# Eight places for returning rows, and scatters of the second half in two of three scan steps

## The chip, the cores and the metric

One core of one Trainium2 chip. The time is the device time of the slowest core in microseconds, here of the only one; the median of the runs is quoted. Engines are named as in the profile: PE (TensorE), DVE (VectorE), ACT (ScalarE), POOL (GpSimd), SP (SyncE). A name ending in q is the instruction queue of an engine, from which DMAs are issued.

## What is computed

The input x has 8 sequences of 512 tokens with 128 channels. After a layer norm two branches run on the same tokens. One is a state-space scan, 512 steps long in the reference, with a layer norm in each step; the other is a mixture of 8 experts, two for each token. The output is x plus the product of both.

```python
def step(state, bc):
    b_t, c_t = bc
    s = state @ A_bar + b_t
    s = _layernorm(s, ln_st_g, ln_st_b)
    return (s, c_t * s)
...
h = _gelu(jnp.einsum('bsd,edh->ebsh', xn, ew1) + eb1[:, None, None, :])
eo = jnp.einsum('ebsh,ehd->ebsd', h, ew2) + eb2[:, None, None, :]
moe_out = jnp.einsum('ebsd,bse->bsd', eo, w_dense)
for i in range(NROT):
    moe_out = moe_out @ expm(gens[i])
...
x = x + s * g
```

Only the two best experts of a token have a weight in `w_dense`, so the kernel computes those two alone.

## The kernel before

**The scan.** Each sequence is cut into 16 segments (`SEG`) of 32 steps (`L`); all 128 segments (8 x 16) are advanced side by side, one on each partition. As the start of a segment is the end of the one before it, the 32 steps are run in five rounds (`ROUNDS`) that improve the starts. The first round begins at its step 12. This makes 148 scan steps, `STEPS`, counted by t from 0. Step t is: VectorE transposes the state (L949), TensorE multiplies it (L1047, 16 small matmuls, semaphore `product`), VectorE finds the root for the layer norm and writes the next state (L961). Rounds end at t = 19, 51, 83 and 115, with two more matmuls and a chain on VectorE (`vector_boundary`).

**The experts.** The 8192 pairs of token and expert are sorted by expert, in two halves of 39 tiles with 128 rows each (`HALF_TILES`, `TILES` = 78). A `scatter` on GpSimd (L1701) is an indirect DMA that writes 128 rows of 129 words (66 KB) to their sorted places in DRAM, `sorted_rows0` for the first half and `sorted_rows1` for the second. There are 64, 32 for each half. Eight go out ahead of the scan (`SCATTER_LEAD`); the others are issued inside the steps, each after that step's `product`.

The tiles are computed in between the scan steps. `SLOT_AT` gives a slot j to four of five steps from t = 26 on, to t = 126. In slot j TensorE does `layer1(j - 2)`, `rows_transpose(j)` and `layer2(j - 3)`, and ScalarE does `gelus(j - 2)`, `rows_transposed(j)` and `rows_copied(j - 3)`. The last of these (L1612) copies the finished tile g from PSUM into place g % `OUT_PLACES` of `rows_out`; it first waits until the scatter that last used this place has landed. From there `rows_back(g)` on GpSimd (L1715), an indirect DMA of 66 KB as well, sends the rows back to the order of the tokens. It stands one step behind the slot. Every third slot GpSimd also computes row numbers (`row_numbers`, L1708). Each engine works through its instructions in the order in which they are written, whatever else is ready.

**SyncE's queue.** `fetch(g)` (L1749) loads the weights of tile g's expert, a record of 290.5 KB, into one of five places once `layer2(g - 5)` is done. It first reads the expert's number into a register. `load_rows(c)` (L1759) loads the sorted rows of three tiles, 193.5 KB, at most three chunks ahead. For c = 0 it waits for all scatters of the first half, for c = 13 (tiles 39 to 41) for all scatters of the second half. SyncE's order is `fetch(35)`, `load_rows(13)`, `fetch(36)`, `fetch(37)`, `fetch(38)`, `load_rows(14)`. Tile 36's record is used by `layer1(36)` in slot 38, at t = 73; tile 39's rows by `rows_transpose(39)` in slot 39, at t = 74.

**Later.** `pull` (L1771) brings the returned rows of a half back into SBUF once all of them have landed, VectorE and ScalarE mix them from t = 82 on, and the output is stored at the end. VectorE also waits for all second-half scatters at t = 116, where the last round begins to write into their source.

Of the kernel before, what the change touches and what calls it, by code (L numbers as in the profile page):

```python
# [19 lines left out]
SEG = 16  # L20
ROUNDS = 5
RECORDS = 5
OUT_PLACES = 5
FIRST_STEP = 12
MAGIC_ROUNDS = 2
TOLERANCE = 1e-5
# [13 lines left out]
def build(nc, I, out):  # L40
    NB, T, H = I["L0_attn_x"].shape
    S = I["L0_attn_A"].shape[0]
    E, _, F = I["L0_ffn_ew1"].shape
    NROT = I["L0_ffn_gens"].shape[0]
    K = F // P
# [5 lines left out]
    Q = NS // HALVES  # L51
# [10 lines left out]
    with ExitStack() as ctx:  # L62
        sems = {}

        def sem(name):
            if name not in sems:
                sems[name] = ctx.enter_context(nc.semaphore(name))
            return sems[name]

        def sb(name, shape, dt=F32):  # L70
            return ctx.enter_context(nc.sbuf_tensor(name, shape, dt))
# [43 lines left out]
        gi = sb("gi", [P, NB, T])  # L115
        rows_out = sb("rows_out", [P, OUT_PLACES, W])
        bias_words = gi[0:3, :, :].rearrange("p b t -> p (b t)")
# [284 lines left out]
        def eb2_split(pool, j):  # L402

            x = eb2r[:, :] if j == 0 else eb2_rest[:, j - 1]
            pool.wait_ge(sem("eb2_copied"), 1)
            if j:
                pool.wait_ge(sem("eb2_parts"), 2 * j)
            pool.tensor_copy(eb2_part[:, j, 0:W], x).then_inc(sem("eb2_parts"), 1)
            if j < 2:
                pool.wait_ge(sem("eb2_parts"), 2 * j + 1)  # L410
                pool.tensor_tensor(eb2_rest[:, j], x, eb2_part[:, j, 0:W], ALU.subtract).then_inc(sem("eb2_parts"), 1)
# [718 lines left out]
        def fallback(eng, one_round, redo):  # L1130

            eng.wait_ge(sem("agreed"), 1)
            settled = eng.value_load(agreed[0:1, 0:1], min_val=0, max_val=1)
            with eng.If(settled < 1):
                if one_round is not None:
                    with eng.Fori(0, SEG) as r:
                        one_round(eng, r)
                redo(eng)
            eng.end_ifs()
# [7 lines left out]
        STEPS = (L - FIRST_STEP) + (ROUNDS - 1) * L  # L1147

        def round_of(t):
            r, k = divmod(t + FIRST_STEP, L)  # L1150
            return r, k, t + 1 + r
# [18 lines left out]
        C_AT = {23: 0, 30: 1, 45: 2, 60: 3, 75: 4, 90: 5, 105: 6, 120: 7}  # L1170
        ROTATED = 14
        SCATTER_LEAD = 8
        MIX_AT = [84, 91, 98, 105, 131, 134, 137, 140]
        VALUES_PER_STEP = [2, 2, 2, 2]
        SUMMED = NB // 2
# [4 lines left out]
        def out_bank(g):  # L1180
            return banks[3 + g % 2][:, 0:W]
# [4 lines left out]
        def value_steps(n):  # L1186
            if n >= SUMMED:
                return MIX_AT[n] + 5, MIX_AT[n] + 8
            return MIX_AT[n] + 5, MIX_AT[n] + 5 + (3 * SUB + VALUES_PER_STEP[n] - 1) // VALUES_PER_STEP[n]

        scaled_rows = [desk[:, i * T:(i + 1) * T].rearrange("p (s h) -> p s h", s=SUB) for i in range(2)]

        def scaled_part(act, n, part):
            _, _, _, a, rest_g = factors(n)
            j = 3 * (n - SUMMED) + part
            if part == 0:
                act.wait_ge(sem("factor"), 5 * n + 5)
            if j >= 2:
                m, p = divmod(j - 2, 3)
                if p == 2:  # L1200
                    act.wait_ge(sem("ffn"), SUMMED + m + 1)
                else:
                    act.wait_ge(sem("summed"), 2 * m + p + 1)
            for s in range(SUB):
                row = pulls[:, n % 4, s, part, 0:P] if part < 2 else abel[:, n, s, :]
                scale = a[:, s, part:part + 1] if part < 2 else rest_g[:, s:s + 1]
                t = act.activation(scaled_rows[j % 2][:, s, :], row, ACT.Copy, scale=scale)
            t.then_inc(sem("scaled"), 1)
# [64 lines left out]
        def vector_mix(dve, n, t):  # L1273

            at = t - MIX_AT[n]
            first, end = value_steps(n)
# [14 lines left out]
        def scalar_mix(act, n, t):  # L1291

            _, u, th, _, _ = factors(n)
            v = values[n % 4]
            if t == MIX_AT[n] - 2:
                if n >= 4:
# [4 lines left out]
                i.then_inc(sem("mix_rows"), 1)  # L1301
            elif t == MIX_AT[n] + 2:
                act.wait_ge(sem("factor"), 5 * n + 3)
# [65 lines left out]
        def residual(pool, again, n):  # L1369
            pool.wait_ge(sem("gated_ssm"), NB * again + n + 1)  # L1370
            pool.tensor_tensor(outb[:, n], outb[:, n], X[:, n * SUB:(n + 1) * SUB, :], ALU.add).then_inc(sem("final_rows"), 1)  # L1371
# [38 lines left out]
        with nc.Block() as block:  # L1410
# [142 lines left out]
            def _(act):  # L1553
# [54 lines left out]
                def rows_copied(g):  # L1608
                    act.wait_ge(sem("rows_done"), g + 1)
                    if g >= OUT_PLACES:  # L1610
                        act.wait_ge(sem(f"rows_out{g % OUT_PLACES}"), 16 * (g // OUT_PLACES))
                    act.copy(rows_out[:, g % OUT_PLACES, :], out_bank(g)).then_inc(sem("rows_copied_out"), 1)  # L1612

# [82 lines left out]
            @block.gpsimd  # L1696
            def _(pool):
                def scatter(i):
                    h, i = divmod(i, 2 * Q)
                    q, j = h * Q + i // 2, i % 2  # L1700
                    pool.indirect_dma_start(sorted_rows[h], bass.IndirectOffsetOnAxis(ap=slots[:, j, q:q + 1], axis=0), sort_rows[:, q, :], None)\  # L1701
                        .then_inc(sem(f"scattered{h}"), 16)

                def row_numbers(c):
                    mine = slice(c * CHUNK, (c + 1) * CHUNK)
                    here = slice((c % 3) * CHUNK, (c % 3 + 1) * CHUNK)
                    pool.wait_ge(sem(f"rows_in{c % 3}"), 16 * (c // 3 + 1))
                    pool.tensor_tensor(token_rows_i[:, mine], row_numbers_in[:, here].squeeze(2), row_shift_i[:, mine], ALU.add)\  # L1708
                        .then_inc(sem("token_rows"), 1)

                def rows_back(g):
                    h = g // HALF_TILES
                    pool.wait_ge(sem("token_rows"), g // CHUNK + 1)
                    pool.wait_ge(sem("rows_copied_out"), g + 1)
                    pool.indirect_dma_start(token_rows[h], bass.IndirectOffsetOnAxis(ap=token_rows_i[:, g:g + 1], axis=0), rows_out[:, g % OUT_PLACES, :], None)\  # L1715
                        .then_inc(sem(f"rows_out{g % OUT_PLACES}"), 16)

                front_gpsimd(pool)
                pool.sem_inc(sem("stored"), 2)
                pool.wait_ge(sem("rows_cleared"), 16 * HALVES)  # L1720
                pool.wait_ge(sem("slots_ready"), 1)
                for i in range(SCATTER_LEAD):
                    scatter(i)
                for t in range(STEPS):
                    r, k, turn = round_of(t)
                    if SCATTER_LEAD + t < 4 * Q:
                        pool.wait_ge(sem("product"), turn)
                        scatter(SCATTER_LEAD + t)
                    if EB2_AT < t <= EB2_AT + 3:
                        eb2_split(pool, t - EB2_AT - 1)  # L1730
                    j = SLOT_AT.get(t - 1)
                    if j is not None and 3 <= j:
                        rows_back(j - 3)
                    j = SLOT_AT.get(t)
                    if j is not None and j < TILES and j % CHUNK == 0:
                        if j == 0:
                            pool.wait_ge(sem("tables"), 10)
                        row_numbers(j // CHUNK)
                for n in range(NB - 3, NB):
                    residual(pool, 0, n)  # L1740
                fallback(pool, pool_round, pool_redo)
# [83 lines left out]
```

## Time and profile before

| | us |
|---|---|
| Median of 3 runs | 410.24 (409.66 to 414.73) |
| The profiled execution's own time | 405.85 |
| Its span, first to last instruction | 404.0 |
| GpSimd's indirect DMAs for the scatters, 64 | 63.8 busy |
| GpSimd's indirect DMAs for the returning rows, 78 | 75.8 busy |
| TensorE's mean granted clock | 0.92 of full speed |

The profile shows one execution. In the timelines a row has a start in microseconds from the start of the span, a duration, the engine, the line and the operation; a bracket behind it gives the idle time of the engine just before and who ended it. DMA rows on GpSimd and SyncE are the time that the engine needs to issue them; the data land later. Step t of the scan can be found by its transpose: L949 occurs 148 times, in the order of t.

### The profile page before, as it was taken

To read this page: it belongs to the slowest core of one execution; us is meant where nothing else is said; L and a number is where in the kernel's file an instruction comes from. 1 tells how busy PE (TensorE), PEld (TensorE's weight loads), DVE (VectorE), ACT (ScalarE), POOL (GpSimd) and SP (SyncE) were. 2 spreads that over 40 slices of the span, in tenths; PEclk is the share of its full clock that TensorE was granted. 3 is DMA by queue.
4 is the path that set the end of the run, shared out by engine and by line. 5 is a ranking of instruction groups with operands and counts; after the bars stand their busy time and mean duration, and the time that the engine had idled before them with its cause. 6 is when DMAs were issued, how large, how long until landed. Compare 5 with 4: busy or idle time off the path is not lost.

```text
span 404.0 us, 11723 instructions
## 1 busy us (share of the span) xinstructions
PE 327.0 (81%) x4029; PEld 244.4 (60%) x4029; DVE 284.0 (70%) x1357; ACT 195.2 (48%) x587; POOL 188.8 (47%) x261
## 2 busy tenths in 40 slices
PE   2897983997787569996997999999997989887670
PEld 1676941775564347875865877877866765443340
DVE  2547589869877547876553666689999567799970
ACT  1217730201322326673636676587775573587510
POOL 8408950725546437777777545345544251000110
PEclk9999986799989959999898999899999899999955
DMA  8199950411110345665564668866656222600001
GB/s 255 22 190 163 135 117 0 130 35 36 41 40 29 140 123 187 231 222 184 189 195 158 219 192 261 280 215 203 210 178 219 79 92 56 228 28 27 28 29 55
DMA packets 44158, 54.81 MB, mean 136 GB/s; under 512 B 6840, under 2 KB 28767, under 8 KB 44095
## 3 DMA queue, kind: packets, MB, share of 16 engines
q1 hardware_dynamic: 38975, 42.52, 37.7%
q0 software_dynamic: 4544, 9.39, 7.1%
q10 hardware_dynamic: 576, 2.10, 1.5%
q8 instruction: 35, 0.57, 0.6%
q14 instruction: 28, 0.23, 0.2%
HBM read 14.15 MB, written 16.63 MB: 76 GB/s over the span
## 4 chain that ended last, share of the span: by engine, by line
PE 40%; DVE 32%; POOL 8%; issue 8%; DMA 6%; ACT 2%; SPq 2%; POOLq 0%; DVEq 0%; ACTq 0%
PE bank L1478 8%; PE bank L1047 7%; PE bank L1488 5%; DVE wT L949 4%; DVE ring L961 3%; DVE roots L914 3%; DMA token_rows<-rows_out,token_rows_i 3%; DVE sqj L938 2%; PE bank L465 2%; PE bank L492 2%; POOL sorted_rows L1701 2%; POOL late L307 2%; DVE xpad L1254 2%; DVE Rho L916 2%; PE bank L1471 2%
## 5 line engine op out<-in xcount | busy, mean ns | idle before, releaser
L1715 POOL DMA_INDIRECT token_rows<-rows_out,token_rows_i x78 | 75.8, 972 | 71.9 <-ACT rows_out L1612 47.6
L1701 POOL DMA_INDIRECT sorted_rows<-late,slots x64 | 63.8, 997 | 56.6 <-PE bank L1047 34.3
L1047 PE MATMUL bank<-Mrep,wT 32*32 32x64 f32 x2368 | 65.9, 226 | 18.8 <-DVE wT L949 18.0
L1047 PEld LDWEIGHTS bank<-Mrep,wT 32*32 32x32 f32 x2368 | 42.2, 108 | 52.6 <-issue 49.3
L1605 ACT ACTIVATE desk<-bank,record 128x128 f32<-128x128 f32 x156 | 48.9, 366 | 36.1 <-PE bank L1478 35.6
L961 DVE SCALAR_TENSOR_TENSOR ring<-bank,Rho,Dv 128x64 f32<-128x64 f32 x112 | 31.6, 282 | 40.5 <-PE bank L1047 38.6
L1478 PE MATMUL bank<-desk,record 128*128 128x128 f32 x312 | 58.5, 313 | 0.0
L1488 PE MATMUL bank<-record,desk 128*128 128x129 f32 x312 | 50.2, 285 | 0.0
L1478 PEld LDWEIGHTS bank<-desk,record 128*128 128x128 f32 x312 | 43.1, 200 | 7.5 <-issue 1.0
L1488 PEld LDWEIGHTS bank<-record,desk 128*128 128x128 f32 x312 | 43.2, 201 | 0.1
L1597 ACT ACTIVATE desk<-bank,cols 128x128 f32<-128x128 f32 x78 | 36.0, 462 | 6.4 <-PE bank L1471 6.4
L1493 PE MATMUL bank<-bias,ones 128*128 128x512 bf16 x116 | 32.5, 385 | 0.0
L1471 PE MATMUL bank<-ident,desk 128*128 128x128 f32 x78 | 22.8, 293 | 11.8 <-DMA desk<-sorted_rows 6.0
L949 DVE STREAM_TRANSPOSE wT<-ring 128x64 f32<-128x64 f32 x112 | 27.5, 245 | 3.6
L1612 ACT COPY rows_out<-bank 128x129 f32<-128x129 f32 x78 | 21.3, 273 | 17.7 <-DMA token_rows<-rows_out,token_rows_i 14.6
L1371 POOL TENSOR_TENSOR xT<-xT,X 128x512 f32<-128x512 f32 x3 | 3.7, 1260 | 53.1 <-DVE xT L1366 53.1
L1471 PEld LDWEIGHTS bank<-ident,desk 128*128 128x128 f32 x78 | 11.8, 151 | 13.1 <-ACT desk L1597 6.3
L938 DVE CUSTOM_DVE_ANT_0 sqj<-ring,guess 128x64 f32<-128x64 f32 x64 | 19.6, 306 | 0.1
L914 DVE SCALAR_TENSOR_TENSOR roots<-z_all 128x1 f32<-128x1 f32 x96 | 16.0, 166 | 3.3
L916 DVE SCALAR_TENSOR_TENSOR Rho<-roots,Rho 128x1 f32<-128x1 f32 x96 | 15.5, 161 | 3.3
L1489 PE MATMUL bank<-record,ones 128*128 128x129 bf16 x78 | 17.8, 228 | 0.0
L594 ACT ACTIVATE gi<-bank,cols 128x512 f32<-128x512 f32 x8 | 5.5, 687 | 22.9 <-PE bank L458 22.9
(328 smaller groups left out, 658.8 us busy)
## 6 DMA issues: line engine op xcount, KB each, us to landing
record<-experts SPq DMA_DIRECT2D x78, 290.5 KB
sorted_rows<-zero_rows SPq DMA_DIRECT2D x2, 2515.5 KB, 26.6
desk<-sorted_rows SPq DMA_DIRECT2D x26, 193.5 KB
pulls<-token_rows SPq DMA_DIRECT2D x8, 516.0 KB, 5.2
X<-in_L_attn_x ACTq DMA_DIRECT2D x4, 512.0 KB, 5.5
out<-xT SPq DMA_DIRECT2D x8, 256.0 KB, 2.0
token_rows<-rows_out,token_rows_i POOLq DMA_INDIRECT x78
experts<-in_L_ffn_ew SPq DMA_DIRECT2D x1, 1024.0 KB, 28.1
```

Of the source, the lines that this page charges most:

```text
L914: dve.scalar_tensor_tensor(out=w_now, in0=z, scalar=linear, in1=z, op0=ALU.add, op1=ALU.mult).then_inc(sem("root_w"), 1)
L949: dve.transpose(wT[:, :], prev).then_inc(sem("state_T"), 1)
L961: dve.scalar_tensor_tensor(out=state(r, k), in0=psY, scalar=Rho[:, k:k + 1], in1=Dv[:, k, :], op0=ALU.mult, op1=ALU.add).then_inc(sem("sta ...
L1047: t = pe.matmul(psY[q], wT[q, 32 * c:32 * c + 32], Mrep[q, c, :], start=(c == 0), stop=(c == 1))
L1471: pe.transpose(bank_in[:, 0:P], rows_in[:, g % (3 * CHUNK), 0:P], ident[:, :]).then_inc(sem("rows_seen"), 1)
L1478: t = pe.matmul(hidden_bank(g)[:, k * P:(k + 1) * P], w[:, k * P:(k + 1) * P], rows_T[:, g % 2, :], start=True, stop=True)
L1488: pe.matmul(o, hidden[:, g % 2, k, :], w[k], start=(k == 0), stop=False)
L1493: pe.matmul(banks[bank][:, :], ones_all3[:, :], bias_all3[:, 1].rearrange("p s h -> p (s h)"), start=True, stop=True)
L1597: act.activation(rows_T[:, g % 2, :], bank_in[:, 0:P], ACT.Identity, scale=col["ln_gamma"], bias=col["ln_beta"]).then_inc(sem("rows_T"), 1)
L1605: t = act.activation(hidden[:, g % 2, k, :], hidden_bank(g)[:, k * P:(k + 1) * P], ACT.Gelu, bias=bias[:, k:k + 1])
L1701: pool.indirect_dma_start(sorted_rows[h], bass.IndirectOffsetOnAxis(ap=slots[:, j, q:q + 1], axis=0), sort_rows[:, q, :], None)\
L1715: pool.indirect_dma_start(token_rows[h], bass.IndirectOffsetOnAxis(ap=token_rows_i[:, g:g + 1], axis=0), rows_out[:, g % OUT_PLACES, :], N ...
```

## The change

Two things. `OUT_PLACES` goes from 5 to 8, so ScalarE waits for the landing of tile g - 8 in place of g - 5. And the second half's scatters are no longer issued one in each step up to t = 55: up to t = 23 nothing changes, from t = 24 on a step divisible by three has none. The last one is then in t = 71. Their number and their data stay the same.

```diff
-OUT_PLACES = 5
+OUT_PLACES = 8
...
         SCATTER_LEAD = 8
+        SCATTER_AT = {}
+        for t in range(STEPS):
+            if SCATTER_LEAD + len(SCATTER_AT) < 4 * Q and (t < 2 * Q - SCATTER_LEAD or t % 3):
+                SCATTER_AT[t] = SCATTER_LEAD + len(SCATTER_AT)
...
-                    if SCATTER_LEAD + t < 4 * Q:
+                    if t in SCATTER_AT:
                         pool.wait_ge(sem("product"), turn)
-                        scatter(SCATTER_LEAD + t)
+                        scatter(SCATTER_AT[t])
```

GpSimd's order before, from t = 53 to the first steps without a scatter. `sorted_rows` rows are scatters, `token_rows` rows are returning rows.

```order
L1701 DMA sorted_rows<-late,slots 4992x129
L1715 DMA token_rows<-rows_out,token_rows_i 9089x129
L1701 DMA sorted_rows<-late,slots 4992x129
L1715 DMA token_rows<-rows_out,token_rows_i 9089x129
L1701 DMA sorted_rows<-late,slots 4992x129
L1715 DMA token_rows<-rows_out,token_rows_i 9089x129
L1708 TENSOR_TENSOR token_rows_i<-desk,row_shift_i 128x3
L1715 DMA token_rows<-rows_out,token_rows_i 9089x129 x3
L1708 TENSOR_TENSOR token_rows_i<-desk,row_shift_i 128x3
```

The last scatter stands behind 20 returns. The same engine after the change, from t = 70, past the last scatter in t = 71 (lines are shifted by 4):

```order
L1705 DMA sorted_rows<-late,slots 4992x129
L1719 DMA token_rows<-rows_out,token_rows_i 9089x129
L1705 DMA sorted_rows<-late,slots 4992x129
L1712 TENSOR_TENSOR token_rows_i<-desk,row_shift_i 128x3
L1719 DMA token_rows<-rows_out,token_rows_i 9089x129 x3
L1712 TENSOR_TENSOR token_rows_i<-desk,row_shift_i 128x3
L1719 DMA token_rows<-rows_out,token_rows_i 9089x129 x3
```

The last scatter now stands behind 33 returns. Between the second return and the last scatter there were 22 scatters, 19 returns (that second one counted) and 6 computations of row numbers; there are now 25, 32 and 10.

SyncE's order has not moved; this is the place in it with the load of tiles 39 to 41, and what it waits for:

```order
L1753 DMA record<-experts 128x581
L1763 DMA desk<-sorted_rows 128x3x129 [waits token_rows,rows_seen,scattered1]
L1750 TENSOR_LOAD expert_of
L1750 ISA x2
L1753 ISA [waits rows_done]
L1753 DMA record<-experts 128x581
```

The record in the first row is tile 35's, the one in the last row tile 36's.

## Rows read from the trace of the kernel before

**Rows 1.** The profile's page: busy time of each engine
```profile
PE 327.0 (81%) x4029; PEld 244.4 (60%) x4029; DVE 284.0 (70%) x1357; ACT 195.2 (48%) x587; POOL 188.8 (47%) x261
```
**Rows 2.** Waits of ACT, 150 to 214 us: total, times, longest
```profile
ACT rows_out L1612 <- DMA token_rows<-rows_out,token_rows_i: 14.6, 9, 3.2
```
**Rows 3.** The chain that ended last, in order of time
```profile
180.52 3.93 DMA token_rows<-rows_out,token_rows_i
```
**Rows 4.** Timeline of POOL, 157 to 223 us
```profile
157.42 0.96 POOL L1715 DMA_INDIRECT token_rows<-rows_out,token_rows_i  x1 [0.30 <-issue]
...
159.95 0.96 POOL L1715 DMA_INDIRECT token_rows<-rows_out,token_rows_i  x1 [0.30 <-issue]
160.94 0.20 POOL L1708 TENSOR_TENSOR token_rows_i<-desk,row_shift_i 128x3 int32<-128x3 int32 x1
161.30 0.99 POOL L1701 DMA_INDIRECT sorted_rows<-late,slots  x1 [0.16 <-issue]
...
209.96 0.96 POOL L1701 DMA_INDIRECT sorted_rows<-late,slots  x1 [0.30 <-issue]
...
222.75 0.96 POOL L1715 DMA_INDIRECT token_rows<-rows_out,token_rows_i  x1 [0.94 <-ACT rows_out L1612]
```
**Rows 5.** Timeline of DVE, transposes of steps 44, 66, 73, 82, 83, 84
```profile
174.12 0.24 DVE L949 STREAM_TRANSPOSE wT<-ring 128x64 f32<-128x64 f32 x1
222.25 0.24 DVE L949 STREAM_TRANSPOSE wT<-ring 128x64 f32<-128x64 f32 x1
233.52 0.25 DVE L949 STREAM_TRANSPOSE wT<-ring 128x64 f32<-128x64 f32 x1
248.85 0.25 DVE L949 STREAM_TRANSPOSE wT<-ring 128x64 f32<-128x64 f32 x1
250.46 0.24 DVE L949 STREAM_TRANSPOSE wT<-ring 128x64 f32<-128x64 f32 x1
254.90 0.25 DVE L949 STREAM_TRANSPOSE wT<-starts 128x64 f32<-128x64 f32 x1
```
**Rows 6.** Timeline of SP's queue; 227.14 is load_rows(13)
```profile
159.43 0.53 SPq L1759 DMA_DIRECT2D desk<-sorted_rows  x1
160.99 4.92 SPq L1749 DMA_DIRECT2D record<-experts  x3
...
174.07 2.96 SPq L1749 DMA_DIRECT2D record<-experts  x3
...
227.14 0.52 SPq L1759 DMA_DIRECT2D desk<-sorted_rows  x1
```
**Rows 7.** DMA issues (KB each, us to landing), and L1701's durations
```profile
pulls<-token_rows SPq DMA_DIRECT2D x8, 516.0 KB, 5.2
out<-xT SPq DMA_DIRECT2D x8, 256.0 KB, 2.0
L1701 POOL DMA_INDIRECT sorted_rows<-late,slots x64: 957/961/1454, 70.3 to 210.0; - x64
DMA to landing us min/median/max: 2.3/2.4/5.6
L1701 POOL DMA_INDIRECT sorted_rows<-late,slots x27: 957/962/997, 149.6 to 210.0; - x27
```
**Rows 8.** Timeline of PE: a slot step at half clock and one at full
```profile
216.78 0.65 PE L1047 MATMUL bank<-Mrep,wT 32*32 32x64 f32 x16
219.69 0.49 PE L1047 MATMUL bank<-Mrep,wT 32*32 32x64 f32 x16
...
232.62 0.43 PE L1047 MATMUL bank<-Mrep,wT 32*32 32x64 f32 x16
234.24 0.43 PE L1047 MATMUL bank<-Mrep,wT 32*32 32x64 f32 x16
234.59 0.71 PE L1478 MATMUL bank<-desk,record 128*128 128x128 f32 x4
```
**Rows 9.** Stretches: length, busy (x) of PE, PEld, DVE, ACT, POOL, PEclk, DMA share, GB/s
```profile
139.00:145.00 6.00, 0.24 (x1) 0.18 (x1) 1.22 (x8) 0.47 (x3) 1.11 (x2) 0.70 0.80 261
145.00:147.00 2.00, 1.59 (x32) 0.96 (x33) 0.94 (x6) 0.92 (x2) 0.92 (x2) 0.50 0.27 77
147.00:151.00 4.00, 4.00 (x41) 3.33 (x34) 3.13 (x19) 1.52 (x6) 2.23 (x4) 0.50 0.11 35
...
213.00:216.00 3.00, 0.32 (x3) 0.12 (x3) 0.95 (x6) 2.83 (x9) 2.39 (x3) 1.00 0.70 209
216.00:220.00 4.00, 4.00 (x48) 3.24 (x48) 1.08 (x6) 2.31 (x8) 3.19 (x5) 0.57 0.35 126
```

## The prediction

> **What bounds the kernel now.** I read the busy times first: TensorE is busy 81% of the span and no other engine over 70% [rows 1], so the question is where TensorE stands still. Then ScalarE's waits between 150 and 214 us: nine times, 14.6 us together, the copy into a returning place (L1612) waits for the row scatter that still holds the place [rows 2]. The same view from 214 us on has no such wait, so all nine lie in the stretch where GpSimd issues both kinds of scatter. The chain that ended last shows one of them: a scatter issued at 180.52 is passed on only 3.93 us later [rows 3].
>
> The timeline of GpSimd says why. From 157.42 us on it issues one indirect DMA after another. Check with the program order: from the second `rows_back` (157.42) to the last `scatter` (209.96) it has 19 + 22 DMAs and 6 short `row_numbers` to pass [rows 4]. A pair with `row_numbers` between them takes 161.30 - 159.95 = 1.35 us; 41 DMAs at 1.266 and 6 times 0.09 give 52.4 us, and 209.96 - 157.42 is 52.5. So GpSimd does not wait at all there: it is a server at 1.27 us a DMA. A group of five scan steps gives it 5 scatters and 4 returns, 9 x 1.27 = 11.4 us; TensorE needs 1.66 us a step when nothing holds it ((248.85 - 222.25) / 16) [rows 5], 8.3 us for the five. GpSimd is the slower one until its scatters end; at 222.75 it waits again for ScalarE [rows 4]. With five places TensorE can't run far ahead, so it takes GpSimd's pace: step 44 starts at 174.12, step 73 at 233.52 [rows 5], 2.05 us a step.
>
> **The change, part by part.**
> *Eight places.* The nine waits go, or nearly: GpSimd's lag may grow to eight slots. Undisturbed, the 29 steps from 44 to 73 take 29 x 1.66 = 48.2 us, and a round boundary inside them (step 52) adds what the one at step 84 adds, 254.90 - 250.46 less 1.66, some 2.8 us [rows 5]. TensorE would come to step 73 at 174.1 + 51.0 = 225.1 in place of 233.5: 8.4 us early. That is the gain on offer, if nothing else stands in the way. Memory apart, this edit adds no instruction.
>
> *The scatters of the second half spread to step 71.* None is removed. GpSimd now gets 10 scatters and 12 returns in 15 steps, 22 x 1.27 = 27.9 us against TensorE's 24.9: still the slower one, by 3 us per 15 steps. So it still never waits, and the time of the last scatter is a count. From the second `rows_back`, whose predecessors in the order are all waiting for TensorE as before and which I therefore leave at 157.42, the order has 32 returns, 25 scatters and 10 `row_numbers` in front of the last scatter: 57 x 1.266 + 10 x 0.09 = 73.1 us, so it starts at 230.5 us, 20.5 us later than before. The 13 returns that now stand before it are 16.5 us of this, three postponed scatters the rest. The fixed spacing excludes more than a microsecond less; more is possible, as a scatter took up to 5.6 us to land in place of 2.4 [rows 7]. I keep -1 to +2 us.
>
> *Who waits for the last scatter.* `load_rows(13)`, the first one of the second half, waits for all 32 scatters of that half, and it stands in SyncE's order directly ahead of `fetch(36)`. Before, the scatters had landed at 212.4 (209.96 + 2.4) and this load went out at 227.14 without waiting for them [rows 6]: 14.7 us of cover, which the move uses up. Behind the waiting load stand `fetch(36)`, (37), (38) and the next load; TensorE needs the first of them in step 73, and ScalarE and the scan stop with it. GpSimd's returns for tiles already computed go on. Now: 230.5 + 2.4 to landing [rows 7] = 232.9; the load's issue takes 0.53; from its end to the next fetch's issue another 1.03 (159.43 + 0.53 to 160.99) [rows 6]: `fetch(36)` at 234.5. Its landing is not listed. From below, the 256 KB store of the output lands in 2.0 us; from above, a 516 KB pull in 5.2 [rows 7]. A record has 290.5 KB, next to the store; I take 2.5 because the 193.5 KB of `load_rows(13)` move just before it. So the record of tile 36 is there at 237.0. TensorE used it at 234.59 (L1478 in step 73) [rows 8]: +2.4 us. The rows of tile 39, needed one step later, leave 1.6 us before the record and are hidden behind it. Further records follow each other at (2.96 - 0.50) / 2 = 1.23 us [rows 6], faster than TensorE's slots, so SyncE catches up and adds nothing.
>
> The Trainium skill, "DMA: Bandwidth & Descriptors", section on the anatomy of a DMA issued from GpSimd, gives each DMA a fixed 2.0 us and the bytes over 436 GB/s. Taken for the record that would be 2.7 us where I take 2.5, and 2.15 us for a 66 KB scatter where the trace has 2.4. An estimate by that page for both makes the gate +2.35 in place of +2.4; the 5.2 of the trace for 516 KB is 2 us above what it gives for that size (3.2), so the trace is not always as quick as the rule, and the upper end stays.
>
> *TensorE stands idle before that.* It comes to step 73 at about 225 and goes on at 237: 12 us without a matmul. In this trace its clock falls to the lower of its levels (1.2 of 2.4 GHz) around such stops: from 139 to 145 us it was busy for 0.24 us, and the granted clock is 0.50 from 145 to 151; from 213 to 216 it was busy for 0.32 us, and the clock is 0.57 from 216 to 220 [rows 9]. A step with a slot takes 219.69 - 216.78 = 2.91 us there and 234.24 - 232.62 = 1.62 at full clock [rows 8], 1.3 us more. The shortest such period held one and a half of these steps, the longest, 145 to 151 and a little more, would hold a little over two. I take 1.7 steps, +2.2 us; the ends are +1.3 and +3.9 (three steps). Before had its own slow period at 216, but that one lies ahead of the gate and gives nothing back.
>
> *After step 74* every step keeps its order. The ScalarE waits were gone there already, so eight places have nothing left to give, and the shift of step 74 runs to the end. The early part up to step 23 is untouched, and so is the first half's load.
>
> **Sum.** The 8.4 us gained before step 73 are spent waiting for the gate, and the gate opens later than before: +2.4 + 2.2 = +4.6 us. On the profiled execution (span 404.0, 405.85 us in all, so 1.85 lie around the span) that is 410.5. The runs shown have a median of 410.24, 4.4 above that execution; the prediction is for such a median: 410.24 + 4.6 = 414.8, 1.1% more. Ends of the sum: GpSimd -1, record 2.0, clock 1.3 gives +2.2; +2, 5.2 and 3.9 give +11.0, an unlikely corner.
>
> **Rivals.**
> *The gate hides nothing (faster).* If the last scatter were issued by about 218.5, the record would be there at 225 and the 8.4 us would stay: 401.8. For it: TensorE really has that much room. Against: GpSimd would have to pass 57 DMAs in 61 us, 1.07 us each, and all of its steady rows have 1.26 to 1.27. 4%.
> *The gate opens just where TensorE was before.* The record lands in 2.0 us, GpSimd is a microsecond early because the returns now come without a late copy, and the clock comes back after one step: +1 or less, 410 to 411.5. 18%.
> *The slow clock stays (slower).* After the gate TensorE could go on at half clock up to the next round boundary at step 84, if short stops between late records keep it from rising: 8 slot steps at 1.3 us, +10.4, with +2.4 for the gate 423. It decides from 4.5 slow steps on, where the sum passes 2%. For it: records 36 to 38 come one by one just then, beside rows and returns, which kept the DMA engines 0.70 busy in the stop at 213 [rows 9]. Against: 1.23 us between records is less than a step, and both periods in the trace ended within 7 us. 13%.
> *The DMAs on GpSimd get longer (slower).* With TensorE undisturbed, VectorE's scan work is denser beside GpSimd's DMAs. The longest scatter of the trace took 1.454 us against a median of 0.961 [rows 7]; were all 57 as long, the gate would open 57 x 0.49 = 28 us later: 443. Against: between 150 and 212 us, with the scan running, the 27 scatters took 957 to 997 ns [rows 7]. 2%.
> The Trainium skill, "SBUF — State Buffer", section "Who interferes with whom", has such a rule: GpSimd is starved of port time for writing its DMAs' descriptors while VectorE holds the port pair that the two share. No row of this stretch shows it at work.
>
> **How the numbers follow.** The forecast (+2 to +8) has 63%, the rivals in their order 4, 18, 13 and 2. About 2% (8.2 us) is what a measurement of this kernel can tell from no change. Faster by more: only the first rival, 0.04. Slower by more: the last two, 0.15. The rest, 0.81: two chances in ten of it lie at or near no change. The range reaches from the second rival to a gate late by most of its bounds (+10.3), and leaves out the far ends: 410.0 to 420.5.
>
> **What would show it.** Right: no ScalarE wait for returning rows; the last second-half scatter at 230 to 232; the load behind it at 233; TensorE idle some 12 us in step 73, ended by the load or record, with a granted clock near 0.5 behind it; the transpose of step 84 some 4 to 5 us later than 254.90. Wrong: GpSimd with idle time between 160 and 230, a spacing other than 1.27, a record in use before 235, or step 84 earlier than before.

## The result, and the profile after

The changed kernel has a median of 413.47 us (20 runs), the kernel before 408.54 (20 runs). The ratio is 1.0129, with a 95% interval of 1.0088 to 1.0169: slower by 1.3%, within the 2% that count as no change. This ratio, and each one below, is taken from each kernel's fast runs alone (those within 1.5% of its fastest), so it differs a little from the quotient of the medians (1.0121). The prediction was 414.8 us, 1.1% more than before. The profiled execution has a span of 407.7 us against 404.0.

ScalarE's waits between 150 and 214 us. The row that stood in [rows 2], a copy waiting for a place, is gone; only a wait for TensorE's result is left at L1616 (L1612 before). The first row is the largest of ScalarE's waits there, at `gelus`:

```profile
ACT desk L1609 <- PE bank L1482: 15.4, 21, 3.9
...
ACT rows_out L1616 <- PE bank L1493: 0.6, 3, 0.2
```

GpSimd's timeline: the second return, the last scatter, and the first return that again had to wait for ScalarE. These answer to [rows 4]:

```profile
158.29 0.96 POOL L1719 DMA_INDIRECT token_rows<-rows_out,token_rows_i  x1 [0.30 <-issue]
...
231.91 0.96 POOL L1705 DMA_INDIRECT sorted_rows<-late,slots  x1 [0.31 <-issue]
...
241.37 0.96 POOL L1719 DMA_INDIRECT token_rows<-rows_out,token_rows_i  x1 [5.86 <-ACT rows_out L1616]
```

The last scatter starts at 231.91, 21.95 us later than in [rows 4]. SyncE's queue is next, its waits first (total, times, longest). A load has waited 12.0 us for scatters, once:

```profile
SPq L1763 <- DMA sorted_rows<-late,slots: 12.0, 1, 12.0
```

In the timeline it is the load at 234.20, `load_rows(13)`, with `fetch(36)` and two more behind it. Nothing leaves the queue between 222.1 and 234.2:

```profile
217.14 4.95 SPq L1753 DMA_DIRECT2D record<-experts  x3
234.20 0.37 SPq L1763 DMA_DIRECT2D desk<-sorted_rows  x1
235.45 2.85 SPq L1753 DMA_DIRECT2D record<-experts  x3
```

TensorE's timeline shows what that costs. The product of step 73 is computed at 229.30; then comes `layer1(36)`, after 8.18 us of idle time that the record ends. The products of steps 74 and 75 follow:

```profile
229.30 0.42 PE L1047 MATMUL bank<-Mrep,wT 32*32 32x64 f32 x16
237.91 1.22 PE L1482 MATMUL bank<-desk,record 128*128 128x128 f32 x4 [8.18 <-DMA record<-experts]
...
240.24 0.65 PE L1047 MATMUL bank<-Mrep,wT 32*32 32x64 f32 x16
...
242.33 0.42 PE L1047 MATMUL bank<-Mrep,wT 32*32 32x64 f32 x16
```

The matmuls behind the stop take 1.22 us where they take 0.71 at full clock [rows 8]. The stretches (columns as in [rows 9]) show the granted clock, 0.50 and then 0.66:

```profile
236.00:238.00 2.00, 0.09 (x1) 0.09 (x1) 0.00 (x0) 0.00 (x0) 0.00 (x0) 0.50 0.70 258
238.00:240.00 2.00, 2.00 (x10) 1.94 (x10) 0.00 (x0) 0.83 (x3) 0.00 (x0) 0.50 0.78 273
240.00:242.00 2.00, 2.00 (x26) 1.59 (x25) 0.57 (x3) 0.59 (x3) 0.63 (x1) 0.66 0.69 230
242.00:244.00 2.00, 2.00 (x24) 1.11 (x23) 1.51 (x10) 1.11 (x5) 0.82 (x3) 1.00 0.70 246
```

And the transposes of steps 44, 73 and 84, beside those in [rows 5]:

```profile
174.92 0.25 DVE L949 STREAM_TRANSPOSE wT<-ring 128x64 f32<-128x64 f32 x1
...
228.65 0.24 DVE L949 STREAM_TRANSPOSE wT<-ring 128x64 f32<-128x64 f32 x1
...
259.75 0.24 DVE L949 STREAM_TRANSPOSE wT<-starts 128x64 f32<-128x64 f32 x1
```

So step 44 is 0.8 us later than before (0.6 of it is there from step 0 on, 88.08 against 87.47), step 73 is 4.9 us earlier, and step 84 is 4.85 us later. The gain is there at step 73; the wait inside that step spends all of it, and more.

### The profile page after: what moved, and what is told of

Its sections match the earlier page's. It is cut to its first block, busy times and chain, and to the rows that moved or that the text cites. A ratio compares the mean times of both kernels' runs of the same rounds, so it can differ in the third digit from the quotient of the medians.

```text
span 407.7 us, 11723 instructions
## 1 busy us (share of the span) xinstructions
PE 326.9 (80%) x4029; PEld 243.9 (60%) x4029; DVE 284.3 (70%) x1357; ACT 195.0 (48%) x587; POOL 189.0 (46%) x261
## 4 chain that ended last, share of the span: by engine, by line
PE 43%; DVE 31%; issue 8%; POOL 6%; DMA 6%; ACT 2%; SPq 2%; DVEq 0%; POOLq 0%; ACTq 0%
PE bank L1482 9%; PE bank L1047 8%; PE bank L1492 6%; DVE wT L949 4%; DVE ring L961 3%; DVE roots L914 2%; DVE sqj L938 2%; PE bank L465 2%; PE bank L492 2%; DVE Rho L916 2%; DVE xpad L1258 2%; PE bank L419 2%; PE bank L1475 2%; POOL sorted_rows L1705 1%; PE bank L1467 1%
## 5 line engine op out<-in xcount | busy, mean ns | idle before, releaser
L1047 PE MATMUL bank<-Mrep,wT 32*32 32x64 f32 x2368 | 66.0, 226 | 18.7 <-DVE wT L949 17.6
L1047 PEld LDWEIGHTS bank<-Mrep,wT 32*32 32x32 f32 x2368 | 42.2, 107 | 52.4 <-issue 49.2
L1497 PE MATMUL bank<-bias,ones 128*128 128x512 bf16 x116 | 33.8, 397 | 0.0
L1616 ACT COPY rows_out<-bank 128x129 f32<-128x129 f32 x78 | 21.4, 274 | 2.8 <-PE bank L1493 2.8
L1497 PEld LDWEIGHTS bank<-bias,ones 128*128 128x128 bf16 x116 | 9.8, 100 | 10.8 <-issue 1.8
```

The costliest lines, as they stand in the source:

```text
L1047: t = pe.matmul(psY[q], wT[q, 32 * c:32 * c + 32], Mrep[q, c, :], start=(c == 0), stop=(c == 1))
L1497: pe.matmul(banks[bank][:, :], ones_all3[:, :], bias_all3[:, 1].rearrange("p s h -> p (s h)"), start=True, stop=True)
```

## The experiments

The theory under test: the time is set by a gate. `load_rows(13)` waits for the last scatter; that scatter's start is a count of DMAs at 1.27 us; SyncE's queue passes the wait on to record 36 and so to TensorE. The main rival: the loss comes with the eight places, or from how much each engine does at once, and the wait is only what the trace names.

Four runs went first to a chip on which the kernel before had a median of 454.6 us (445.6 to 457.6, 11 runs). They are told at the end of this section; the same kernels were run again on other chips, and those runs decide.

### One part alone: eight places

```diff
-OUT_PLACES = 5
+OUT_PLACES = 8
```

> Edit: eight places alone, again, as the first run of it had a kernel before of 454.6 us beside it, 46 us over the median known, with TensorE waiting for its own instructions in the profile. Gate theory, where the kernel before takes 403 to 412 us: last scatter near 210 us, ScalarE's waits for places under 6 us, step 73 4 to 8 us earlier than before; ratio 0.980 to 0.990. Rival (places bring nothing or cost): 1.00 to 1.01.

Measured: 403.02 us against 407.59, ratio 0.990 (0.983 to 0.997). The scatter that ends the row is again at its old time, and from 150 to 300 us ScalarE waits for no place; this is GpSimd's row, and then all of TensorE's waits between 150 and 300 us:

```profile
210.04 0.95 POOL L1701 DMA_INDIRECT sorted_rows<-late,slots  x1 [0.31 <-issue]
```
```profile
PE bank L1052 <- DVE ends L971: 3.5, 2, 1.9
PE bank L1471 <- ACT desk L1597: 0.9, 1, 0.9
PE bank L1478 <- DMA record<-experts: 0.7, 2, 0.5
PE bank L1047 <- DVE wT L949: 0.5, 1, 0.5
```

Step 73 comes at 227.5 us, 6.0 us earlier than before, and step 84 still is 6.1 us earlier. The eight places gain what this experiment expected (4 to 8 us), less than the 8.4 of the prediction; the ratio stands at the weak end of the expected range. The trace shows why in part: of the 6.1 us 3.1 are left at step 147 (377.0 against 380.1), and the span ends 3.7 us earlier. Step 119 loses 1.3 us and step 147 another 1.85; ahead of the latter the granted clock is 0.56 from 370 to 375 us, where the kernel before has 1.00 up to 380. Whether another execution would lose them too is not tested.

### The other part alone: the spread

The changed kernel with

```diff
-OUT_PLACES = 8
+OUT_PLACES = 5
```

> Edit: the spread alone, five places, again. Gate theory: last scatter at 231 to 233 us, record of tile 36 at 237 to 238, ratio 1.009 to 1.017 as the changed kernel. Rival (the loss comes with the places): under 1.005.

Measured: 412.81 against 407.59, ratio 1.013 (1.007 to 1.020), the changed kernel's own. The last scatter starts at 234.22 and the record is used at 240.27, both later than expected (231 to 233, 237 to 238): this execution, of 415.0 us, began its tile loop later, see the table below. The wait for the record is there, longer:

```profile
240.27 1.22 PE L1482 MATMUL bank<-desk,record 128*128 128x128 f32 x4 [10.72 <-DMA record<-experts]
```

The rival falls: the loss comes with the spread alone, and next to it five or eight places make no difference. Even with five places ScalarE waits for none in this kernel, as GpSimd has fewer DMAs in each step, and step 73 comes at 228.5 us, where the changed kernel has 228.65. So the sum of the parts is not the whole: -1.0% and +1.3% apart, +1.3% together. Either part alone takes ScalarE's waits away, so next to the spread the places have nothing to add; and what is gained ahead of the gate, by either, is spent at the gate.

### The count changed: three of four steps

```diff
-... t < 2 * Q - SCATTER_LEAD or t % 3):
+... t < 2 * Q - SCATTER_LEAD or t % 4):
```

> Edit: the changed kernel with scatters in three of four steps from step 24 on. The last one is in step 66 with 29 returns ahead of it in place of 33, and 62 in place of 67 row of DMAs and row numbers. Gate theory: it starts 4 x 1.27 = 5 us earlier than the changed kernel's, near 227, the record of tile 36 comes near 233, and the ratio to before is 0.997 to 1.004. Rival (the price is not set by the count): ratio 1.009 or more, as the changed kernel.

Measured: 406.90 against 406.90, ratio 0.999 (0.995 to 1.003). GpSimd, then SyncE, then TensorE:

```profile
226.88 0.96 POOL L1705 DMA_INDIRECT sorted_rows<-late,slots  x1 [0.31 <-issue]
```
```profile
229.18 0.37 SPq L1763 DMA_DIRECT2D desk<-sorted_rows  x1
230.33 2.95 SPq L1753 DMA_DIRECT2D record<-experts  x3
```
```profile
233.06 1.22 PE L1482 MATMUL bank<-desk,record 128*128 128x128 f32 x4 [5.34 <-DMA record<-experts]
```

Each of these times is 4.9 to 5.1 us earlier than in the changed kernel, where the count gives 5.2. Record 36 is used 1.5 us earlier than in the kernel before, and the clock behind the stop takes that back: step 84 comes 0.8 us later (255.71). This execution took 410.31 us, 3.4 over its kernel's median. This is the sharpest test, since one number of the edit changes: four returns fewer stand ahead of the last scatter, and the ratio is 1.4 points under the changed kernel's, though taken on another chip.

### The queue changed: two fetches ahead of the load

The changed kernel, SyncE's loop:

```diff
+                LATE = HALF_TILES - 3 * CHUNK
                 for g in range(TILES):
                     if g + RECORDS < TILES:
                         fetch(g + RECORDS)
-                    if g % CHUNK == 0 and g // CHUNK + 3 < TILES // CHUNK:
+                    if g == LATE + 2:
+                        load_rows(LATE // CHUNK + 3)
+                    if g != LATE and g % CHUNK == 0 and g // CHUNK + 3 < TILES // CHUNK:
                         load_rows(g // CHUNK + 3)
```

> Edit: fetches of records 36 and 37 ahead of the load of tiles 39 to 41, again. Gate theory: step 74's transpose of rows resumes at about 236.5 us in place of a resumption of step 73 at 237.9, step 75 comes 3 to 5 us earlier than in the changed kernel, ratio 1.000 to 1.006. Rival (the order of the queue is not what costs): 1.009 to 1.017.

Measured: 410.07 against 407.59, ratio 1.0057 (1.0013 to 1.0102), inside the expected range. TensorE now passes step 73 and stops one step later, at the rows of tile 39:

```profile
237.83 0.48 PE L1475 MATMUL bank<-ident,desk 128*128 128x128 f32 x1 [7.45 <-DMA desk<-sorted_rows]
...
239.21 0.65 PE L1047 MATMUL bank<-Mrep,wT 32*32 32x64 f32 x16
```

Tile 39's rows were used at 237.83, 1.3 us later than expected; 0.9 of it is the later last scatter. The product of step 75 (second row) comes 6.4 us after the start of the last scatter (232.79), in the changed kernel 10.4 us (231.91 to 242.33). By step 80 2.7 of these 4.0 us are left, counted from the last scatter (248.5 against 250.3 at the transpose): the half clock now falls on large products behind step 75's (two 128x512 matmuls of L1447, 2.08 us where the changed kernel takes 1.13). So two waits stand behind one gate, the last scatter: the record's, and behind it that of tile 39's rows, which comes up once the record's is gone. About half of the loss stays with it.

### The clock: TensorE kept busy in the stop

The changed kernel with 36 matmuls more, 128x512 each, whose results nobody reads:

```diff
                     if t in SLOT_AT:
                         j = SLOT_AT[t]
+                        if j == HALF_TILES - 1:
+                            keep_warm(36, 1)
                         if 2 <= j < TILES + 2:
                             layer1(j - 2)
```

> Edit: the changed kernel with 36 more matmuls in slot 38, in the idle time before record 36; again, as the first run of it had a kernel before of 454.6 us beside it. Clock theory: granted clock near 1.0 from the arrival of record 36 on, and step 75 follows 1 to 2 us sooner after that arrival; the ratio is 0.002 to 0.005 under that of the changed kernel on the same chip. Rival (the clock is not what costs): the same ratio within 0.001.

> The changed kernel itself, beside e4r_kept_warm on one chip as its yardstick: ratio to before 1.009 to 1.017 by every theory.

Measured on one chip: 409.95 with them and 412.18 without, against 407.57 for the kernel before; ratios 1.0029 (0.9985 to 1.0073) and 1.0090 (1.0049 to 1.0131). TensorE with them (35 of the 36 are in the trace):

```profile
227.43 7.72 PE L1497 MATMUL bank<-bias,ones 128*128 128x512 bf16 x35 [0.16 <-issue]
236.66 0.71 PE L1482 MATMUL bank<-desk,record 128*128 128x128 f32 x4 [1.52 <-DMA record<-experts]
...
239.56 0.42 PE L1047 MATMUL bank<-Mrep,wT 32*32 32x64 f32 x16
```

```profile
236.00:240.00 4.00, 3.33 (x53) 2.83 (x53) 1.05 (x6) 2.11 (x8) 0.69 (x1) 1.00 0.69 230
```

The granted clock is 1.00 behind the stop, and from record 36 to the product of step 75 it takes 2.90 us (236.66 to 239.56) in place of 4.42 (237.91 to 242.33): the clock's price is 1.5 us in that execution of the changed kernel. It is not the same in each. From the first use of record 36 to the transpose of step 80:

| execution | us | over the kernel before |
|---|---|---|
| before (no stop) | 10.89 | |
| kept warm | 10.89 | 0.0 |
| changed | 12.42 | 1.5 |
| changed, again | 13.04 | 2.2 |
| three of four | 13.24 | 2.4 |
| spread alone | 13.73 | 2.8 |

With TensorE kept busy the price is gone to the last hundredth. In the ratios the difference is 0.6%, a little over the expected 0.2 to 0.5 (2.2 us, as in the execution of the changed kernel on this chip, would be 0.5%), and the two intervals overlap; the traces are the better evidence. The rival that VectorE's chain is what is late there falls by the 2.90.

### Scatters forward in place of back

Two in each of steps 1, 3, 5, 6, 7 and 9, three in each of steps 24 to 26, one in the others, up to step 43; with eight places, and with five:

```diff
+            last = min(first + (2 if t in (1, 3, 5, 6, 7, 9) else 3 if t in (24, 25, 26) else 1), 4 * Q)
+            SCATTER_AT[t] = range(first, last)
```

> Edit: eight places; the second half's scatters are moved forward in place of back: two in each of steps 1, 3, 5, 6, 7 and 9, three in each of steps 24 to 26, where GpSimd has idle time, and one in the others. The last one is in step 43 with 10 returns ahead of it in place of 33. Gate theory: the last scatter starts before 185 us, nothing waits for it, ScalarE has almost no wait for a place (under 2 us), step 73 comes 5 to 9 us earlier than in the kernel before; ratio to before 0.975 to 0.988. Rival (GpSimd's lateness only moves elsewhere, to the start of the tile loop or to the later returns): ratio over 0.992.

> Edit: as e5_early_8 with five places. If the surplus of DMAs on GpSimd inside the tile loop is what fills the places, moving 12 scatters (15 us of GpSimd) forward takes most of the waits away without more places: ratio 0.980 to 0.993, and what eight places add to it is under 0.6%. Rival (five places are too few at any pace of GpSimd): ratio over 0.995, with ScalarE waiting more than 8 us for places.

Measured: with eight places 401.61 against 406.90, ratio 0.988 (0.981 to 0.995); with five 404.73, ratio 0.986 (0.977 to 0.995). GpSimd's last scatter of the first of them, and ScalarE's waits for places in the second, 3.7 us in place of 14.6:

```profile
183.83 0.95 POOL L1707 DMA_INDIRECT sorted_rows<-late,slots  x1 [0.30 <-issue]
```
```profile
ACT rows_out L1618 <- DMA token_rows<-rows_out,token_rows_i: 3.7, 3, 2.2
```

With eight places ScalarE has no wait for one. One expectation was missed: step 73 comes at 229.85 us with eight places, 3.7 earlier than before in place of 5 to 9. The execution was 1.7 us late from step 0 on (89.16 against 87.47), and the granted clock fell to 0.50 behind the round boundary of step 52, as in item 3 of the account below.

Both are faster than both kernels of the case, by less than 2%. The surplus of DMAs on GpSimd inside the tile loop filled the places; fewer DMAs there or more places to hold them each take most of the waits away. Of the three ways to faster (places alone 0.990, forward with eight 0.988, with five 0.986) none can be told from the others. Forward has a price of its own: the row numbers for the first tiles are computed at 147.56 in place of 144.85 us, behind the nine scatters of steps 24 to 26; 1.7 of these 2.7 us are the later start of the execution.

### The count over all executions

For each execution whose profile was taken on a chip other than the slow one: the start of the second return, the DMAs and row numbers ahead of the last scatter by the program's order, that count at 1.266 and 0.09 us, the time measured, and how long after the last scatter's start tile 36's first matmul started, where it waited for the record.

| kernel | second return | DMAs, row numbers | count gives | measured | last scatter to record in use |
|---|---|---|---|---|---|
| before | 157.42 | 41, 6 | 52.4 | 52.5 | no wait |
| changed | 158.29 | 57, 10 | 73.1 | 73.6 | 6.00 |
| changed, again | 161.15 | 57, 10 | 73.1 | 73.1 | 6.07 |
| spread alone | 161.15 | 57, 10 | 73.1 | 73.1 | 6.05 |
| kept warm | 157.34 | 57, 10 | 73.1 | 73.2 | 6.17 |
| fetches first | 159.71 | 57, 10 | 73.1 | 73.1 | waits for rows |
| three of four | 158.93 | 53, 9 | 67.9 | 68.0 | 6.18 |
| places alone | 157.61 | 41, 6 | 52.4 | 52.4 | no wait |
| forward, eight | 159.52 | 19, 3 | 24.3 | 24.3 | no wait |
| forward, five | 159.54 | 19, 3 | 24.3 | 24.3 | no wait |

### The chip on which all was slower

> Edit: eight places, scatters one in each step as before. Gate theory (the load of tiles 39 to 41 waits for the last scatter, whose start is a count of DMAs at 1.27 us): the last scatter stays near 210 us, its landing near 212.4 is still ahead of the load's turn, and the nine waits of ScalarE shrink from 14.6 us to under 6; step 73 comes 4 to 8 us earlier than in the kernel before and this is kept: ratio to before 0.980 to 0.990. Rival (the eight places are what costs, or bring nothing): ratio 1.00 to 1.01.

> Edit: five places, scatters in two of three steps from step 24 on. Gate theory: GpSimd has the same DMAs ahead of the last scatter as in the changed kernel, so it starts at 231 to 233 us and the record of tile 36 comes at 237 to 238; ScalarE's waits for places may come back but cost nothing, and the ratio to before is that of the changed kernel, 1.009 to 1.017. Rival (each scatter less per step helps TensorE, the loss comes with the places): the ratio is under 1.005.

> Edit: the changed kernel with SyncE's fetches of records 36 and 37 put ahead of the load of tiles 39 to 41, that waits for the last scatter. Gate theory: step 73 no longer waits for its record, TensorE goes on to step 74 and stands at the rows of tile 39 in place of the record; these land at about 233.9 + 0.5 + 2.4, some 236.5 us, where the changed kernel resumed step 73 at 237.9 and had two slot steps in front of it. So step 75 comes 3 to 5 us earlier than in the changed kernel, and the ratio to before is 1.000 to 1.006. Rival (the wait for the record is only what the trace names, the time is set by GpSimd's returns or by the slow clock): ratio 1.009 to 1.017 as in the changed kernel.

> Edit: the changed kernel with 36 more matmuls of 128x512 in slot 38 on TensorE, ahead of the first matmul that needs record 36; their results are not used. They take 36 x 0.216 = 7.8 us of the 8.2 us in which TensorE stood idle. Clock theory (1.5 us of the loss are the two steps at half clock behind the idle time): granted clock 1.0 from 238 on, step 75 1 to 2 us earlier than in the changed kernel against step 73's record, ratio 0.003 to 0.005 below that of the changed kernel. Rival (the clock costs nothing since the scan's chain on VectorE is what is late there): same ratio as the changed kernel.

Measured, against 454.63 us for the kernel before: places alone 455.68, ratio 1.015 (1.005 to 1.026); spread alone 458.34, 1.023 (1.012 to 1.033); fetches first 460.39, 1.019 (1.001 to 1.037); kept warm 464.87, 1.035 (1.019 to 1.051). No ratio lies in its expected range. By these ratios eight places would be a loss, but they rest on two of the eleven runs of the kernel before (445.58 and 451.28 us); the medians give 1.002, 1.008, 1.013 and 1.023, so a change of sign is not shown. The traces show a different bound. TensorE's waits of "places alone" between 150 and 300 us, where "issue" means that no other engine and no DMA was waited for (columns as above), and a scatter on GpSimd that waited for something the trace calls remote:

```profile
PE bank L1047 <- issue: 21.3, 19, 1.8
```
```profile
234.04 0.96 POOL L1701 DMA_INDIRECT sorted_rows<-late,slots  x1 [1.05 <-remote]
```

In the traces from the other chips nothing waits for "remote", and TensorE's issue waits at L1047 are 0.4 us or less in all; the scatter that started at 234.04 here started at 210.04 there. On this chip the count does not hold, and the theory's numbers can't be read from it. In the spread kernels there the last scatter came 103 to 109 us after the second return, where the count gives 73, with many waits for TensorE and ScalarE. One reading, which an expectation above states as if the profile showed it, is that the engines get their own instructions late; the profile shows only that nothing it records was waited for. That 36 matmuls more made the worst run fits the reading, but it was not tested, and what slows that chip stays open.

## Why the prediction was right

1. *GpSimd as a server at 1.27 us a DMA.* Right: nine executions of the table agree with the count within 0.1 us, the changed kernel's first within 0.6. There GpSimd, which was to wait for nothing, waited twice for TensorE's product, behind the round boundary of step 52, while TensorE ran at half clock:

```profile
194.37 0.96 POOL L1705 DMA_INDIRECT sorted_rows<-late,slots  x1 [0.40 <-PE bank L1047]
...
197.28 0.98 POOL L1705 DMA_INDIRECT sorted_rows<-late,slots  x1 [0.46 <-PE bank L1047]
```

   The steady gaps are 0.30 and, behind row numbers, 0.16 us, so the two cost 0.4. The last scatter was said to start at 230.5 and did at 231.91; 0.87 of the difference is the later start of the second return.
2. *The gate.* Right in place, and near in price. From the last scatter's start to the record in use I had 6.5 us (230.5 to 237.0); five executions show 6.0 to 6.2. Record 36 was used at 237.91 in place of 234.59, +3.3 us against +2.4 said: the last scatter was 1.4 later than said, the stretch behind it 0.5 shorter.
3. *The gain on offer.* Mis-sized: TensorE was to come to step 73 8.4 us early and came 4.9 early (228.65 against 233.52). It started from step 44 0.8 us later, and the 29 steps from there took 53.7 us, not 51.0. Most of this lies behind the round boundary, which I had priced by the boundary at step 84. The stretches of the changed kernel show half clock for some 6 us; the last two rows are those of the spread alone, where the clock stayed up:

```profile
190.00:192.00 2.00, 1.78 (x8) 1.78 (x9) 0.69 (x7) 0.00 (x0) 1.39 (x3) 0.54 0.10 33
192.00:194.00 2.00, 2.00 (x25) 1.53 (x24) 0.21 (x1) 1.24 (x4) 1.66 (x2) 0.50 0.23 72
194.00:196.00 2.00, 2.00 (x13) 2.00 (x10) 1.02 (x6) 0.75 (x3) 1.32 (x2) 0.50 0.56 203
```
```profile
194.00:196.00 2.00, 2.00 (x32) 1.75 (x31) 1.20 (x8) 1.24 (x5) 1.39 (x3) 1.00 0.15 41
196.00:198.00 2.00, 2.00 (x31) 1.60 (x29) 1.29 (x9) 1.52 (x6) 1.70 (x2) 1.00 0.69 252
```

   TensorE stood 2.10 us at this boundary in both. In the three kernels with the spread whose clock stayed at 1.00 behind it (spread alone, fetches first, three of four) the 29 steps took 50.7, 50.7 and 50.3 us, close to the 51.0 said; why the clock fell in one execution and not in another stays open. The prediction also gave the end of ScalarE's waits to the eight places alone; the spread alone ends them too. The term stood outside the sum, since the gate decides however early TensorE comes; so the idle time was 8.2 us and not 12, and the total did not move.
4. *The clock behind the stop.* 1.5 us in the profiled execution against 2.2 said, and 2.2, 2.4 and 2.8 in three others that stop in step 73 (table above): 2.2 was a fair middle, all within the bounds (1.3 to 3.9). In the first the clock was back some 4 us after the record.
5. *The sum.* +4.6 was said; step 84 is 4.85 us later, 0.6 of it from the start of the execution. That the sum fits so well is in part luck: the gate cost 0.9 us more than said, the clock 0.7 less. The shift was to run to the end and did not: at step 100 it is 3.9 us, as the clock fell behind the boundary of step 84 in the kernel before (0.50 from 254 to 256 us) and not in the changed one, and the span ends 3.7 later. In the medians it is 413.47 - 408.54 = +4.9; the interval of the ratio reaches from 3.6 to 6.9 us, so that 4.6 comes so near is luck as well.
6. *The rivals.* "The gate opens just where TensorE was" did not happen in the changed kernel; the one with three of four steps has its outcome (0.999), by an earlier last scatter. "The gate hides nothing" is what places alone are. The slow clock did not stay, and GpSimd's DMAs did not get longer: the table's spacing is the same in all kernels, also where ScalarE waited for no place.

The level of 414.8 leaned on three runs of the kernel before with a median of 410.24; twenty have 408.54. This level was 1.7 us too high and the difference 0.3 too low, so the forecast stands 1.3 us above the result.

## What to carry to other kernels

To relieve an engine that is late, moving its work to later steps helps only as long as nobody comes to wait for the end of that work; find who waits for the last piece, and in whose queue that wait stands, before the first piece is moved. In a queue worked through in order, the finish time of a piece is the number of things put ahead of it times their spacing, and that count can be read from the program before anything is run. It holds while the queue never runs dry and what bounds it stays the same: two short waits cost the changed kernel 0.4 us, and on the slow chip the count failed. A gain ahead of such a gate is no gain: here -1.0% and +1.3% made +1.3%.

## What was not expected of the hardware

The clock went down behind shorter stops than I had looked at: at the round boundary of the changed kernel TensorE stood 2.1 us, and the granted clock was 0.54 and 0.50 for the 6 us from 190 on (rows above). The length of the stop does not decide it: ten executions stood 1.9 to 2.4 us at that boundary, and behind it the clock fell to about half in six and stayed at 1.00 in four, the spread alone with the same 2.10 us among them. Behind the stop before record 36 it fell each time: in the changed kernel it was 1.00 until 234 us, 0.64 on average in the next two and 0.50 from 236 on. Keeping TensorE busy through the stop kept it at 1.00.

One chip ran all kernels 11% slower, with waits that no other engine or DMA ended. By the medians, the gain of eight places was not to be seen there: 1.002, against a ratio of 0.990 elsewhere.
